# Modulation and lag matmuls placed two at a time in the upper and lower 64 rows of TensorE

## What is computed

```python
ctx = causal_ema(x, tau_ctx)
gated = x * sigmoid(concat([x, ctx]) @ Wg.T + bg)
h1 = gelu(x @ Wn1.T + bn1)                       # 32 hidden
mod = 0.5 + sigmoid(h1 @ Wn2.T + bn2)            # 32 decays d, for every time step
traces = [causal_ema(gated * mod[..., d], tau[d]) for d in range(32)]
temporal = einsum('dbtc,dc->btc', traces, softmax(blend, axis=0))
soma = gelu(x @ Wsoma.T + bsoma)
x = x + layernorm((soma * sigmoid(temporal @ Wtemp.T + btemp)) @ Wout.T)
...
x = x + attention(x)                             # 16 heads, dense or over 32 given keys
```

## Time and profile before

| | |
|---|---|
| median of 3 runs | 341.86 us (341.52 to 347.49) |
| the profiled execution | 341.25 us, its span from first to last instruction 339.3 us |
| PE busy | 317.3 us (93%) |
| DVE busy | 291.6 us (86%) |
| POOL, ACT busy | 224.3 us (66%), 215.0 us (63%) |
| front and first step | 0 to 47.6 us |
| steps two to seven | 47.5 to 167.0 us, between 19.6 and 20.8 us each |
| end and attention | 167.0 to 339.3 us |

### The profile page before, as it was taken

How to read it: one execution, slowest core, us unless ns; L and a number is a source line. 1 busy time by engine, 2 the same in 40 slices (tenths; PEclk the granted TensorE clock), 3 DMA queues, 4 the chain that set the end, 5 groups by cost and what they waited for, 6 DMA issues and landing times. The chain is left out here.

```text
span 339.3 us, 10025 instructions
## 1 busy us (share of the span) xinstructions
PE 317.3 (93%) x3333; PEld 211.4 (62%) x3333; DVE 291.6 (86%) x1500; ACT 215.0 (63%) x458; POOL 224.3 (66%) x279
## 2 busy tenths in 40 slices
PE   7998888999999999999988799999999999999995
PEld 2545254573756557474535576777787877787873
DVE  3895699999898999988788866999999999999982
ACT  6760225566455656555716787788888878888863
POOL 3254164535355453625537768799999999999990
PEclk9996799999999999999999999999999999999999
DMA  6600002015060421301551244565555354301011
GB/s 190 198 3 0 31 0 65 32 49 93 2 139 2 90 52 53 88 0 53 69 74 28 39 93 79 84 120 139 127 100 122 92 123 101 84 5 34 2 34 33
DMA packets 29155, 23.08 MB, mean 68 GB/s; under 512 B 2736, under 2 KB 27824, under 8 KB 29104
## 3 DMA queue, kind: packets, MB, share of 16 engines
q1 hardware_dynamic: 29104, 22.44, 30.3%
HBM read 7.75 MB, written 2.10 MB: 29 GB/s over the span
## 5 line engine op out<-in xcount | busy, mean ns | idle before, releaser
L1566 POOL TENSOR_TENSOR arena<-arena,neg_max 128x512 f32<-128x512 f32 x128 | 129.6, 1042 | 14.3 <-DVE neg_max L1437 13.8
L1437 DVE CUSTOM_DVE_ANT_0 arena<-ps,arena 128x128 f32<-128x128 f32 x512 | 113.6, 286 | 11.6 <-issue 5.8
L1076 ACT ACTIVATE arena<-ps 128x512 f32<-128x512 f32 x128 | 69.6, 597 | 9.0 <-PE ps L775 8.9
L1514 POOL TENSOR_TENSOR arena<-arena 128x448 f32<-128x448 f32 (+6 forms) x56 | 41.1, 735 | 48.5 <-DVE arena L1268 45.1
L775 PE MATMUL ps<-ident_sb,arena 128*128 128x128 f32 x512 | 68.2, 276 | 0.0
L775 PEld LDWEIGHTS ps<-ident_sb,arena 128*128 128x128 f32 x512 | 56.5, 141 | 7.0 <-issue 4.3
L1501 POOL TENSOR_TENSOR arena<-decay_a,arena 128x192 f32<-128x192 f32 x32 | 20.0, 655 | 36.2 <-ACT arena L920 36.2
L1437 DVE DVE_READ_ACCUMULATOR2_ANT neg_max<- 128x1 f32 x512 | 42.4, 83 | 0.0
L791 PE MATMUL ps<-arena 128*32 128x128 f32 x1024 | 41.2, 279 | 0.0
L791 PEld LDWEIGHTS ps<-arena 128*32 128x32 f32 x1024 | 24.0, 109 | 6.9 <-issue 0.3
L761 PE MATMUL ps<-arena 48*128 48x128 bf16 x512 | 25.4, 219 | 3.0 <-DVE neg_max L1437 3.0
(11 more groups left out here) (164 smaller groups left out, 584.2 us busy)
## 6 DMA issues: line engine op xcount, KB each, us to landing
arena<-q_parts SPq DMA_DIRECT2D x96, 64.0 KB
arena<-k_parts SPq DMA_DIRECT2D x96, 64.0 KB
arena<-in_x SPq DMA_DIRECT2D x16, 256.0 KB, 3.7
arena<-in_xt SPq DMA_DIRECT2D x8, 256.0 KB, 3.6
out<-arena SPq DMA_DIRECT2D x7, 256.0 KB, 3.5
arena<-in_consts SPq DMA_DIRECT2D x1, 420.0 KB, 3.7
w_sb<-in_w SPq DMA_DIRECT2D x1, 384.0 KB, 5.2
w_sb<-in_w SPq DMA_DIRECT2D x1, 192.0 KB, 4.3
```

The costliest lines, as they stand in the source:

```text
L1076: act.activation(probT[q % PT_RING], ps[1][:, q % 2, :], ACT.Exp, scale=-1.0)\
L1437: dve.tensor_tensor_reduce(out=neg_t[q % NT_RING][:, cs], in0=ps[0][:, score_bank(c) + slot, cs], in1=nbias[n % 2], scale=1.0, scalar=3.0e ...
L1514: pool.tensor_tensor(a, a, pr_, ALU.add).then_inc(s["lag_added"], 1)
L1566: pool.tensor_tensor(t4, t4, neg_max[:, n % 2, 4 * z:4 * z + 4].unsqueeze(2).broadcast_to([P, 4, P]), ALU.subtract).then_inc(s["shifted"], 1)
```

## The change

- `f_modulation`: the four matmuls use 64 rows each. Rows 0 to 63 write bank 0, rows 64 to 127 bank 1, alternating, 256 columns in each. ACT's tanh reads both banks in one instruction. It now also waits for ACT's copy of `b_cross` (`cross_ready`), which had stood before `f_soma`.
- `f_soma` comes behind `f_gate_x` and waits for the modulation's tanh, since it writes bank 0.
- The lags of groups 1 to 7 go in pairs, `f_lag_pair`: L526's matmul for both lags at full height, then the second matmul of the first lag in rows 64 to 127 and that of the second lag in rows 0 to 63. `lag_b` and `mod_pb` hold a copy of their upper half in the lower one.
- For that ACT gets a new copy in each step, `f_mod_low` (64 partitions by 512, bf16), ahead of the tanh of the gate, and makes `f_mod_part1b` ahead of `f_soma`. The prologue's weights get one more copy on ACT (`w_b1`), `w_mid` and `w_b2` on DVE cover 96 partitions in place of 32, and two memsets go.
- The order: lag 2 and 3 come behind `b_crossT` together; lag 6 comes behind `b_out`, and 6 and 7 ahead of `c_v`, which is the last in the step.

Left out below: semaphore names, `front`'s renaming of `f_lags` to `first_lags`, and the waits for `w_b1` in DVE's `front`.

```diff
@@ -73,7 +73,7 @@
              "key_no", "idx_f", "mask_f", "idx_plus", "idx_masked", "kept_bias"] + \
             [f"hot{j}" for j in range(K_SPARSE)] + ["count", "cnt_one", "cnt_none"]
-ACT_STEPS = ["exp_tau", "softplus", "exp_table", "exp_blend", "lt", "apow", "decay_p", "decay_a", "exp_u", "w_b3", "w_a1", "w_a3"]
+ACT_STEPS = ["exp_tau", "softplus", "exp_table", "exp_blend", "lt", "apow", "decay_p", "decay_a", "exp_u", "w_b3", "w_a1", "w_a3", "w_b1"]
 def vec(name):
...
@@ -437,9 +437,9 @@
             def f_soma(i, m):
                 u = m % 2
-                if not at_start(i, m, 2):
-                    pe.wait_ge(s["cross_ready"], grp(i, m, 1, -1))
+                if not at_start(i, m, 1):
+                    pe.wait_ge(s["modT_tanh"], grp(i, m, 1, 1))
                 if at_start(i, m, 1):
                     pe.wait_ge(s["w_loaded"], 16)
                 pe.matmul(bank(u, 0), wt["wsoma"], xT[u], start=True, stop=True).then_inc(s["soma_ps"], 1)
...
@@ -477,8 +477,15 @@
                 if not at_start(i, m, 2):
                     pe.wait_ge(s["temporal_ready"], grp(i, m, 1, -1))
-                for b in range(GB):
-                    mm = pe.matmul(bank(u, 1)[:, b * P:b * P + P], wn2_row[:, b, :], h1T[u], start=True, stop=True)
+                    pe.wait_ge(s["cross_ready"], grp(i, m, 1, -1))
+                if at_start(i, m, 1):
+                    pe.wait_ge(s["soma_ready"], 1)
+                two_banks = ps[u][:, 0:2, :]
+                for b in (0, 2, 1, 3):
+                    half, c0 = slice(64 * (b // 2), 64 * (b // 2) + 64), (b % 2) * P
+                    mm = pe.matmul(two_banks[:, b // 2, c0:c0 + P], wn2_row[half, b, :], h1T[u][half, :],
+                                   start=True, stop=True)
                 mm.then_inc(s["modT_ps"], 1)
             def f_modulation_n(i, m):
...
@@ -499,33 +506,44 @@
                 pe.wait_ge(s["gated_ready"], grp(i, m, 1, 1))
                 turned(bank(u, 2), gT[u], "gn_ps")
-            def f_lags(i, m, lags):
-                u = m % 2
+            def first_lags(u, lags):
                 for lag in lags:
                     if lag == 0:
-                        pe.wait_ge(s["soma_ready"], grp(i, m, 1, 1))
-                        if at_start(i, m, 1):
-                            pe.wait_ge(s["vec_step"], vec("w_lag"))
-                            pe.wait_ge(s["modT_tanh"], 1)
-                        else:
-                            pe.wait_ge(s["mod_part3"], grp(i, m, 1, 1))
-                            pe.wait_ge(s["mod_part1b"], grp(i, m, 1, 1))
-                            if at_start(i, m, 2):
-                                pe.wait_ge(s["vec_step"], vec("w_b2"))
-                                pe.wait_ge(s["act_step"], scal("w_a3"))
+                        pe.wait_ge(s["soma_ready"], 1)
+                        pe.wait_ge(s["vec_step"], vec("w_lag"))
+                        pe.wait_ge(s["modT_tanh"], 1)
                     if lag == 1:
-                        pe.wait_ge(s["modn_ready"], grp(i, m, 1, 1))
+                        pe.wait_ge(s["modn_ready"], 1)
                     if lag >= 2:
-                        pe.wait_ge(s["prod_ready"], grp(i, m, Q, lag - 1))
-                    if at_start(i, m, 1):
-                        pe.matmul(bank(u, lag % 2), w_lag[0:D, lag, :], thd[u][0:D, :], start=True, stop=True)\
-                            .then_inc(s["lag_ps"], 1)
-                        continue
-                    pe.matmul(bank(u, lag % 2), lag_a[:, lag, :], mod_pa[u][:], start=True, stop=False)
-                    pe.matmul(bank(u, lag % 2), lag_b[:, lag, :], mod_pb[u][:], start=False, stop=True)\
+                        pe.wait_ge(s["prod_ready"], lag - 1)
+                    pe.matmul(bank(u, lag % 2), w_lag[0:D, lag, :], thd[u][0:D, :], start=True, stop=True)\
                         .then_inc(s["lag_ps"], 1)
+            def f_lag_pair(i, m, lag):
+                u = m % 2
+                if lag == 0:
+                    pe.wait_ge(s["soma_ready"], grp(i, m, 1, 1))
+                    pe.wait_ge(s["mod_part3"], grp(i, m, 1, 1))
+                    pe.wait_ge(s["mod_part1b"], grp(i, m, 1, 1))
+                    if at_start(i, m, 2):
+                        pe.wait_ge(s["vec_step"], vec("w_b2"))
+                        pe.wait_ge(s["act_step"], scal("w_b1"))
+                else:
+                    pe.wait_ge(s["prod_ready"], grp(i, m, Q, lag - 1))
+                pe.matmul(bank(u, 0), lag_a[:, lag, :], mod_pa[u][:], start=True, stop=False)
+                if lag == 0:
+                    pe.wait_ge(s["modn_ready"], grp(i, m, 1, 1))
+                else:
+                    pe.wait_ge(s["prod_ready"], grp(i, m, Q, lag))
+                pe.matmul(bank(u, 1), lag_a[:, lag + 1, :], mod_pa[u][:], start=True, stop=False)
+                if lag == 0:
+                    pe.wait_ge(s["mod_low_ready"], grp(i, m, 1, 1))
+                pe.matmul(bank(u, 0), lag_b[64:128, lag, :], mod_pb[u][64:128, :], start=False, stop=True)\
+                    .then_inc(s["lag_ps"], 1)
+                pe.matmul(bank(u, 1), lag_b[0:64, lag + 1, :], mod_pb[u][0:64, :], start=False, stop=True)\
+                    .then_inc(s["lag_ps"], 1)
             def decayed(u, b, first, last):
                 return mod_a[u][:, b * W + first * D:b * W + last * D]
...
@@ -660,17 +678,17 @@
                 f_modulation(i, m)
                 f_gate_ctx(i, m)
                 f_modulation_n(i, m)
-                f_lags(i, m, range(0, 2))
+                first_lags(m, range(0, 2))
                 f_modulation(i, m + 1)
                 f_gated(i, m)
...
...
@@ -678,8 +696,8 @@
                     f_hidden(i, m + 1)
                     b_carries(i, m)
                     f_modulation(i, m + 1)
+                    f_gate_x(i, m + 1)
                     f_soma(i, m + 1)
-                    f_gate_x(i, m + 1)
                     f_context(i, m + 1)
                 b_locals(i, m)
                 if not closes:
...
@@ -691,29 +709,28 @@
                     f_modulation_n(i, m + 1)
                     f_gate_ctx(i, m + 1)
                     c_x1T(i, m - 1)
-                f_lags(i, m + 1, range(0, 2))
+                f_lag_pair(i, m + 1, 0)
                 if closes:
                     c_k(i, m - 1)
                     b_cross(i, m)
                 f_gated(i, m + 1)
                 if closes:
                     c_less(i, m - 1, 1, 0)
-                f_lags(i, m + 1, range(2, 3))
                 b_crossT(i, m)
-                f_lags(i, m + 1, range(3, 4))
+                f_lag_pair(i, m + 1, 2)
                 if closes:
                     c_q(i, m - 1)
                 b_gate(i, m)
                 if closes:
                     c_less(i, m - 1, 1, 1)
                     c_less(i, m - 1, 0, 0)
-                f_lags(i, m + 1, range(4, 7))
+                f_lag_pair(i, m + 1, 4)
                 if closes:
                     c_less(i, m - 1, 0, 1)
                 b_out(i, m)
+                f_lag_pair(i, m + 1, 6)
                 if closes:
                     c_v(i, m - 1)
-                f_lags(i, m + 1, range(7, Q))
             def repeat(times):
...
@@ -899,7 +916,7 @@
             def f_modulation(i, m):
                 u = m % 2
                 act.wait_ge(s["modT_ps"], grp(i, m, 1, 1))
-                act.activation(thd[u], bank(u, 1), ACT.Tanh, bias=hb[:, 2:3], scale=0.5).then_inc(s["modT_tanh"], 1)
+                act.activation(thd[u].rearrange("p (k n) -> p k n", k=2), ps[u][:, 0:2, 0:2 * P], ACT.Tanh, bias=hb[:, 2:3], scale=0.5).then_inc(s["modT_tanh"], 1)
             def f_mod_part1(i, m):
...
@@ -912,6 +929,13 @@
                 u = m % 2
                 act.wait_ge(s["modT_tanh"], grp(i, m, 1, 1))
                 act.activation(mod_pb[u][64:96, :], thd[u][64:96, :], ACT.Copy).then_inc(s["mod_part1b"], 1)
+            def f_mod_low(i, m):
+                u = m % 2
+                act.wait_ge(s["mod_part1b"], grp(i, m, 1, 1))
+                act.wait_ge(s["mod_part3"], grp(i, m, 1, 1))
+                act.activation(mod_pb[u][0:64, :], mod_pb[u][64:128, :], ACT.Copy).then_inc(s["mod_low_ready"], 1)
             def f_modulation_n(i, m):
...
@@ -992,6 +1017,8 @@
                 act.wait_ge(s["vec_step"], vec("w_rest"))
                 for r0 in (32, 96):
                     act.activation(lag_a[r0:r0 + 32], w_rest[r0:r0 + 32], ACT.Copy).then_inc(s["act_step"], 1)
+                act.wait_ge(s["vec_step"], vec("w_b2"))
+                act.activation(lag_b[32:64], w_lag[32:64], ACT.Copy).then_inc(s["act_step"], 1)
                 act.wait_ge(s["vec_step"], vec("lag_c"))
                 f_mod_part1b(i, m + 1)
...
@@ -1002,15 +1029,17 @@
                     f_modulation_n(i, m + 1)
                     f_context(i, m + 1)
                     b_cross(i, m)
+                    f_mod_low(i, m + 1)
                     f_gate(i, m + 1)
```

(13 more changed lines are left out.)

13 lines of the change are left out of this document (7 added, 6 removed).

## The result

The changed kernel took 351.73 us in the median of 4 runs (346.61 to 352.60), the kernel before 341.69 beside it; the ratio is 1.022 with a 95% interval of 1.017 to 1.027. Six more runs, beside the last experiments, gave 349.02 us and 1.014 (1.010 to 1.019). The prediction had 343.8 us and a range to 347.0. It had the sign and missed the size.

The account below looks back on a forecast made before the run. PE and DVE, both nearly full, were taken to bound each step through one knot of waits. Each step would be 0.27 us longer, seven steps 1.9, put on the median 341.86: 343.8 us, range 339.9 to 347.0.

Parts of the forecast that it names:

- The way back from the halves: PE's change from half-row matmuls back to full height: 0.11 us more, bounds nothing and 0.21.
- What bounds it: One step: PE and DVE nearly full, their two waits one knot; floor 19.58 - 0.55 = 19.03 us.
- The price of the height, inwards: PE's change from full-height to half-row matmuls: 0.09 us more than the pitch of 0.22.
- Four pairs in a step: nothing won: Lag pairs on PE: each goes from 0.86 to 0.85 us, changes of height included, so no gain.
- `f_mod_low`: New ACT copy in each step: 0.63 us, bounds 0.3 and 0.7; tanh and x1T's copy begin 0.11 later.
- The chain: Walk through one step from `f_mod_low` through `c_k`, `b_gate` and `b_out` to `c_moments`: step 0.27 us longer.
- the likeliest case: Rival A, the walk's slightly longer step: 343.8 us, range 341.9 to 345.4, chance 0.60.
- the front up to 26 us is led by DVE's tables, and the earlier modulation saves nothing there.: The front, ahead of the steps: DVE's tables lead, so the earlier modulation saves nothing.
- rival D: Granted clock: a second low stretch, 4.8 us, 348.6 us (chance 0.09), or the front's stretch vanishes, 339.0 (0.04).
- B: Rival: matmuls saved bring steps down to DVE's floor, 7 x -0.55 = -3.9, 338.0 us; chance 0.17.
- C: Rival: halves don't run together, or shared tanh and copy queue up; 4.9 us more, 346.8; chance 0.10.
- The other signs: Profile signs of being right: steps 19.8 to 19.9 us, 0.3 into the halves, `b_carries` waiting 0.4, `c_k` waiting for x1T's copy.

## Why the prediction was wrong

Two steps of the sum failed. The clock in the front was put at nothing, and the early fall cost up to 8.5 us there. The way back from the halves was put at 0.11 us, and it is 0.20 ahead of an f32 pair, which with two small terms makes a step 0.46 us longer and not 0.27. Point by point:

- **What bounds it** held. The knot of lag 4, lag 6, `b_out` and `c_moments` is there: untying it alone gave 1.5%. The floor of 19.03 was a little too high: 18.91 was reached.
- **The price of the height, inwards** (0.09) held: 0.31 - 0.22 = 0.09, and 0.10 at lag 6. **Outwards** it did not. I took 0.11 from matmuls with one short instruction each; ahead of a long f32 pair it is 0.10 of gap and another 0.10 in the pair's own time, 0.20, which is the upper bound that I had named (0.21) and not used. At full height the loads of 0.10 us run under a matmul on the same 128 rows (105.60), and where the rows change, from 128 to 64, the load of 0.09 us does not run ahead (90.36).
- **"Four pairs in a step: nothing won"** should have read: 0.19 lost, on pairs 2 and 6, which are on the chain.
- **`f_mod_low`**: cost 0.63 as said: its bf16 input did not make it shorter than L914 with f32 input (0.63 in the kernel before). But `c_k` came 2.06 us after the end of VectorE's third part (86.51 - 84.45) where I had 1.99 and the kernel before 1.88.
- **The chain** had the right links in the right order. Counted from the end of the third part: `b_gate` 6.80 before, 6.98 by the walk, 7.20 measured (91.65 - 84.45); `c_moments` 11.45, 11.72, 11.91. The first half of the walk was short by 0.22: 0.07 at `c_k`, 0.06 in `b_crossT` (0.49 us where I had 0.43) and 0.09 for the way back from the halves; from there on it was right to 0.03. A step was 0.46 longer and not 0.27. Six of them were 3.28 us longer and not 1.6; the first alone is 0.99 longer, which the walk of a later step could not show. That alone would have been 341.7 + 3.3 = 345.0 us, in the likeliest case's range; the kernel with the front's modulation at full height measured 344.87.
- **The step that failed first was never worked out: "the front up to 26 us is led by DVE's tables, and the earlier modulation saves nothing there."** True of the order of work, false of the clock. The clock was in the prediction only as rival D, at 0.09, tied to more idling in the steps and to chance. I had the row with the low stretch and asked what it cost, not what stood in front of it. Right in front of it stand matmuls of 32 rows (L523, 2.71 us from 26.12), and the change took some of the few with 128 away and opened a wait of 0.35 us there. The long fall cost 8.5 us at the first mark, more than D's 4.8 for a second stretch. It did not come in every run: the four runs of ten at 346.2 to 346.6 us lie inside the range.
- **B** was rightly low: VectorE waits 0.66 us ahead of lag 6's product. **C** fell: the halves start within 0.01 us of each other. **D** had its sign, a clock under 1.00 after 40 us, but gave another reason. That more idling in the steps brings such a stretch was a guess of mine and is not shown: in the changed kernel TensorE stands still for 1.17 us of a step of 20.03, and the clock is 1.00 from 47 to 177 us. The three profiled runs with a stretch at 58.6 to 64.4 us have waits of 1.15 to 1.16 and 0.68 to 0.90 us right ahead of it; the kernel with the front's modulation at full height has 1.16 and 0.90 us there and no stretch.
- **The other signs**: 0.31 us from the second full matmul to the first half, no wait of TensorE for lag 4, 0.38 us of waiting ahead of `b_carries` and 0.62 ahead of `c_k` all came as written. Steps of 19.8 to 19.9 us did not.

## What to carry to other kernels

Two bf16 matmuls of 512 columns side by side in half the rows saved one pitch of 0.22 us here, and the changes of height cost 0.09 going in and 0.10 to 0.20 coming out; one pair per change was a loss (1.81 us against 1.72). Whether several pairs in a row pay was not tried. Before halving anything on TensorE, look in the profile for stretches at the lower clock (0.50 here), and at what stands ahead of them, waits as well as work: here two groups of matmuls shortened from 1.16 to 0.71 us ahead of such a stretch cost up to 8.5 us. And when two engines wait for each other once in a step, look first for the order that unties them; here that brought 1.5%, and the halved matmuls nothing.
